# Blocks 1 to 7 of x: transposed by DMA as 16-bit halves and joined by GpSimd, in place of TensorE transposes

## The reference, cut to what matters

```python
x = x + L0(x)            # recurrent layer, below
x = x + L1(x)            # one linear layer, its weights chosen per batch row by an index
x = L2(x)                # adapter (512 -> 128 -> 512, relu) added to x, then a layer norm
x = x + L3(x)            # one linear layer, chosen per batch row
# L0:
ctx    = ema(x, tau)                              # over time, per channel
wg     = sigmoid([x, ctx] @ Wg.T + bg);  gated = x * wg
mod    = 0.5 + sigmoid(gelu(x @ Wn1.T) @ Wn2.T)   # two rows per token
trace_d = ema(gated * mod_d, tau_d)               # d = 0, 1
temporal = blend of the two traces
out    = (gelu(x @ Wsoma.T) * sigmoid(temporal @ Wtemp.T)) @ Wout.T
L0     = layernorm(out)
```

## Time and profile before

| what | value |
|---|---|
| median of 3 runs | 788.96 us (787.5 to 789.58) |
| the profiled execution | 787.42 us |
| its span, first to last instruction | 785.6 us |
| PE, DVE, ACT, POOL busy | 98%, 68%, 41%, 13% of the span |

### The profile page before, as it was taken

One profiled execution on the slowest core, in us unless ns is written; L12 is line 12 of the kernel. 1 busy time (PEld: TensorE's weight loads), 2 busy tenths in 40 slices (PEclk: granted clock), 3 DMA queues, 4 the chain that ended last, 5 costly groups with the idle time before them and its releaser, 6 DMA issues. The chain is left out here.

```text
span 785.6 us, 10804 instructions
## 1 busy us (share of the span) xinstructions
PE 767.6 (98%) x3628; PEld 628.3 (80%) x3628; DVE 533.8 (68%) x782; ACT 323.8 (41%) x525; POOL 101.4 (13%) x227
## 2 busy tenths in 40 slices
PE   5999999999999999999999999998999999999997
PEld 4888888888888888888888888776888888888885
DVE  3598894694695595595596587746775776657645
ACT  4444426226225315315325424656453544535332
POOL 2000020021012003003003004324001020110110
PEclk9999999999999999999999999999999999999999
DMA  7413004004004004102102514443142241313102
GB/s 222 167 55 108 27 1 161 28 0 161 27 0 160 27 0 146 41 0 111 76 0 81 136 53 157 146 146 141 41 148 70 105 147 41 121 63 111 40 28 82
DMA packets 32480, 66.29 MB, mean 84 GB/s; under 512 B 10800, under 2 KB 11824, under 8 KB 30400
## 3 DMA queue, kind: packets, MB, share of 16 engines
q1 hardware_dynamic: 32224, 65.87, 24.2%
q0 software_dynamic: 224, 0.00, 0.0%
HBM read 40.67 MB, written 25.20 MB: 84 GB/s over the span
## 5 line engine op out<-in xcount | busy, mean ns | idle before, releaser
L557 PE MATMUL pc<-x_h,wg_h 128*128 128x512 f32 x224 | 89.2, 398 | 0.0
L559 PE MATMUL pc<-x_h,wg_l 128*128 128x512 f32 x224 | 88.0, 393 | 0.0
L558 PE MATMUL pc<-x_l,wg_h 128*128 128x512 f32 x224 | 87.2, 389 | 0.0
L1292 DVE TENSOR_TENSOR_SCAN stage_b<-alpha,carry,stage_b 128x512 f32<-128x512 f32 x64 | 78.4, 1267 | 0.0
L999 ACT ACTIVATE ctx_t<-ctx_t,col_bg 128x512 f32<-128x512 f32 x32 | 23.2, 724 | 97.4 <-DVE ctx_t L1272 97.4
L1227 DVE TENSOR_TENSOR x_l<-x_t,x_h 128x512 fp32r<-128x512 f32 x32 | 22.2, 692 | 47.5 <-ACT x_t L949 47.5
L653 PE MATMUL pm<-t_h,wt_h 128*128 128x512 f32 x128 | 51.4, 402 | 0.0
L557 PE MATMUL pm<-wo_h,s_h 128*128 128x512 f32 x128 | 50.6, 395 | 0.7 <-DVE s_l L1251 0.7
L559 PE MATMUL pm<-wo_h,s_l 128*128 128x512 f32 x128 | 50.5, 394 | 0.0
L558 PE MATMUL pm<-wo_l,s_h 128*128 128x512 f32 x128 | 50.4, 394 | 0.0
L655 PE MATMUL pm<-t_h,wt_l 128*128 128x512 f32 x128 | 50.3, 393 | 0.0
(11 more groups left out here) (226 smaller groups left out, 1881.1 us busy)
## 6 DMA issues: line engine op xcount, KB each, us to landing
xt_scratch<-x_t SPq DMA_DIRECT2D x8, 1024.0 KB, 4.0
n_scratch<-stage_a SPq DMA_DIRECT2D x8, 1024.0 KB, 4.7
ctx_t<-xt_scratch SPq DMA_DIRECT2D x16, 512.0 KB, 6.4
x_tok<-in_x_dram SPq DMA_DIRECT2D x30, 256.0 KB, 2.8
out_dram<-x_tok SPq DMA_DIRECT2D x28, 256.0 KB, 2.0
s_h<-n_scratch SPq DMA_DIRECT2D x12, 512.0 KB, 4.9
mod<-mod_scratch SPq DMA_DIRECT2D x8, 512.0 KB, 3.5
stage_b<-in_L_cond_weight_dram SPq DMA_DIRECT2D x2, 1024.0 KB, 5.5
```

Source lines behind the costliest of these rows:

```text
L557: nc.tensor.matmul(acc, ah, bh, start=start and q == 0, stop=False)
L558: nc.tensor.matmul(acc, ah, bl, start=False, stop=False)
L559: last = nc.tensor.matmul(acc, al, bh, start=False, stop=stop and q == n - 1)
L1292: nc.vector.tensor_tensor_scan(tr[:, m % 2, :], alpha[:, 1 + d:2 + d].to_broadcast([P, BLK]), tr[:, m % 2, :], carry[:, D - d, m:m + 1], A ...
```

## The change

Only block 0 is still transposed by TensorE. For block i+1, SP issues one DMA transpose of its 512 by 1024 halves (16 bits each) from DRAM into `x_pairs`, in which even partitions hold the low halves and odd partitions the high halves of a channel (`turn_x` of SP). Four DMAs within SBUF sort them into `x_planes` (`spread_x`). GpSimd then reads a chunk's two planes and writes them as whole words into `x_t`, with one 1024-element copy of 16-bit elements (`weave_x`), behind a small instruction that writes `gone`. ScalarE makes `x_h` from `x_t` in four instructions a block in place of eight, and VectorE makes `x_l` chunk by chunk. The copy of chunk c may start when `gate_x(i, c)` has read the old chunk and the old block is stored. `c_h`, `c_l` of phase 2 are gone; x2's parts go to `t_h`, `t_l` for block 0 and to `s_h`, `s_l` for the others, and the normalised rows are read back into `x_pairs` and `x_planes`.

```diff
+    x_halves = t["x"].rearrange("b n e -> (b n) e").bitcast(U16)
-        c_h, c_l = sb("c_h", [P, NC, BLK], F32R), sb("c_l", [P, NC, BLK], F32R)
+        x_pairs, x_planes = sb("x_pairs", [P, NC, BLK]), sb("x_planes", [P, NC, BLK])
+        gone = sb("gone", [P, NC])
...
+        def x2_parts_of(i):
+            return (t_h, t_l) if isinstance(i, int) and i == 0 else (s_h, s_l)
...
+            def turn_x(i):
+                after(sp, x_spread, (i - 1) * 64)
+                sp.dma_start(pairs16, x_halves[bass.ds(i * BLK, BLK), :], transpose=True).then_inc(x_turned, 16)
+
+            def spread_x(i):
+                sp.wait_ge(x_turned, i * 16)
+                after(sp, x_woven, (i - 1) * NC)
+                for half in range(2):
+                    for s in range(2):
+                        sp.dma_start(planes16[64 * s:64 * s + 64, :, half, :],
+                                     pairs16[half::2, s::2, :]).then_inc(x_spread, 16)
...
             def step(i):
-                load_x(i + 1, 0)
-                load_x(i + 1, 1)
+                turn_x(i + 1)
                 store_xt(i)
+                spread_x(i + 1)
                 spread_mod(i)
-                load_x(i + 1, 2)
-                load_x(i + 1, 3)
                 store_n(i - 1)
...
+            def weave_x(i, c):
+                pool.wait_ge(x_spread, i * 64)
+                pool.wait_ge(xt_out, i * 16)
+                pool.wait_ge(gated, i * NC + (c + 1 - NC))
+                nc.gpsimd.tensor_tensor(gone[:, c:c + 1], keep[:, 0:1], keep[:, 1:2], ALU.mult)
+                nc.gpsimd.tensor_copy(words16[:, c, :, :], planes16[:, c, :, :].rearrange(
+                    "p w q -> p q w")).then_inc(x_woven, 1)
...
             def step(i):
-                temp_product(i - 1, (0, 1))
-                turn_x(i, 2)
-                turn_x(i, 3)
-                temp_product(i - 1, (2, 3))
+                temp_product(i - 1, range(NC))
                 h1_product(i)
...
+            def x_hi_part(i, c):
+                act.wait_ge(x_woven, i * NC + (c + 1 - NC))
+                if c == 0:
+                    act.wait_ge(soma_mm, i * NC)
+                nc.scalar.activation(x_h[:, c, :], x_t[:, c, :], ACT.Identity).then_inc(xcopy, 1)
...
                 norm_stats(i - 1, 1)
-                scan_traces(i, 2)
                 norm_stats(i - 1, 2)
                 norm_stats(i - 1, 3)
+                scan_traces(i, 2)
                 temporal_lo(i, 1)
```

More of the change, by code:

```diff
@@ L262, in store_xt @@
             def store_xt(i):
-                sp.wait_ge(xcopy, i * TILES + TILES)
+                if isinstance(i, int) and i == 0:
+                    sp.wait_ge(xcopy, TILES)
+                else:
+                    sp.wait_ge(x_woven, i * NC)
                 sp.dma_start(block_of(xt_scratch, i), x_t[:, :, :]).then_inc(xt_out, 16)
@@ L372, in _ @@
                         sp.dma_start(seq[n][:, b, :], cols_of(t[src], lang(b))).then_inc(lw_in, 16)
[L373 to L378, removed]
+            sp.wait_ge(x_spread, LAST * 64)
+            sp.wait_ge(n_out, 32)
+            for half in range(2):
+                load_n_half(0, x_pairs[:, 2 * half:2 * half + 2, :], half)
+            for half in range(2):
+                load_n_half(1, x_planes[:, 2 * half:2 * half + 2, :], half)
             spread_mod(LAST)
@@ L450, in _, with norm_scale @@
             pool.wait_ge(pool_step, 5)
-            def norm_scale(at, j, have_mv, done):
+            def norm_scale(at, j, have_mv, done, between=None):
                 v, y, q = newton[:, 0, :], newton[:, 1, :], newton[:, 2, :]
@@ L490, in carry_traces, with step @@
                                         ALU.mult).then_inc(tr_carry, 1)
-            def step(i, first=False, ends=False):
+            def weave_x(i, c):
[5 more added lines that the diff above has]
+                    "p w q -> p q w")).then_inc(x_woven, 1)
+            def step(i, first=False, ends=False, last=False):
                 k = 0 if ends else 1
                 carry_context(i, k)
[L496 to L500, removed]
+                carry_traces(i, 0, k)
+                if not last:
+                    weave_x(i + 1, 0)
+                    weave_x(i + 1, 1)
+                carry_traces(i, 1, k)
+                if not last:
+                    weave_x(i + 1, 2)
+                if first:
+                    weave_x(i + 1, 3)
+                    carry_traces(i, 2, k)
+                else:
+                    norm1_scale(i - 1, lambda: carry_traces(i, 2, k))
+                carry_traces(i, 3, k)
+                if not (first or last):
+                    weave_x(i + 1, 3)
             pool.wait_ge(setup_v, 4)
@@ L506, in _ @@
             step(PER_SEQ - 1, ends=True)
-            with pool.Fori(PER_SEQ, NBLK) as i:
+            with pool.Fori(PER_SEQ, LAST) as i:
                 step(i)
+            step(LAST, last=True)
             def add_eye(chunks, first, eye):
@@ L589, in ready, with turn_x @@
                 pe.wait_ge(w_lo, W_BEFORE[n] + W_COUNT[n])
[L591 to L599, removed]
+            def turn_x(k):
+                pe.wait_ge(x_in[k] if k < 2 else first_in[k - 2], 16)
                 if k >= 2:
-                    pe.wait_ge(xcopy, i * TILES + (k - 1))
-                src = x_first(k) if isinstance(i, int) and i == 0 else x_tok[:, k % 2, :]
-                turn(pt[k % 2], [src[:, out_cols(c)] for c in range(NC)]).then_inc(tx_done, 1)
+                    pe.wait_ge(xcopy, k - 1)
+                turn(pt[k % 2], [x_first(k)[:, out_cols(c)] for c in range(NC)]).then_inc(tx_done, 1)
             def of_x(wh, wl, at, o):
@@ L617, in u_chunk @@
             def u_chunk(i, m):
+                if m == 0:
+                    after(pe, soma_g, i * NC - 2)
                 if m == 1:
@@ L733, in _ @@
             step_end(1, first=True)
-            next_x(1)
-            with pe.Fori(2, LAST) as i:
+            with pe.Fori(2, NBLK) as i:
                 step(i)
-                next_x(i)
-            step(LAST)
             def turn_l3(b, k, bank):
@@ L779, in w1_product @@
                 wh, wl = w1_w(b)
+                c_h, c_l = x2_parts_of(i)
                 pairs = [(wh[:, c, :], wl[:, c, :], c_h[:, c, :], c_l[:, c, :]) for c in range(NC)]
@@ L1029, in traces_part @@
                 soma_gelu(i, 3)
-                if not last:
-                    copy_x(i + 1, 0)
                 temporal_hi(i, 3)
                 if not last:
-                    copy_x(i + 1, 1)
+                    for c in range(NC):
+                        x_hi_part(i + 1, c)
             def step(i, last=False):
-                copy_x(i, 2)
-                copy_x(i, 3)
                 gates(i - 1, lambda: hidden(i))
@@ L1342, in traces_part @@
                 blend_traces(i, 3)
-                if not last:
-                    x_lo_part(i + 1, 0)
                 temporal_lo(i, 3)
                 if not last:
-                    x_lo_part(i + 1, 1)
+                    for c in range(NC):
+                        x_lo_chunk(i + 1, c)
             def step(i, last=False):
-                x_lo_part(i, 2)
-                x_lo_part(i, 3)
                 gates(i - 1, lambda: hidden_lo(i))
```

108 lines of the change are left out of this document (48 added, 60 removed).

## The result

The changed kernel takes 798.37 us in the median (4 runs, 797.18 to 798.74), the kernel before 788.23 (4 runs, 785.42 to 789.58): a ratio of 1.0124, with a 95% interval of 1.0106 to 1.0143. It is 1.2% slower: the direction was forecast, but it is 10 us and not 50. The profiled execution took 798.66 us, its span 796.9.

The account below looks back on a forecast made before the run. PE, busy 98%, was taken as the bound, beside a second chain as long as the step (slack 1.0 us). 787.4 + 37.5 + 8.1 − 0.9 = 832.1 us, with the clock 839; range 775 to 866.

Parts of the forecast that it names:

- The price of the copy, w: Time of one 1024-element GpSimd copy, taken as 2.9 us, with bounds of 1.3 and 4.8.
- The sum's form: Whole kernel time as 768.3 + 22w, without the clock loss; 832.1 us at the forecast w.
- The turns: TensorE transposes of x: 0.88 us a group, 14 groups removed, 12.3 us saved if nothing else moves; PE step 58.8.
- Mutual exclusion: A VectorE instruction with two SBUF inputs and a GpSimd one reading SBUF block each other for a whole instruction.
- The first rival: GpSimd's copies share freely with VectorE; 9.9 us saved, 777.5 us; chance 0.14.
- The chain: Work freeing PE's banks each step: copies +3w − 0.5, scans −2.46, norm_scale +2.3 to 2.4; together 3w − 0.6 longer.
- The wait forecast on the banks: PE waits 3w − 0.7 = 8.0 us each step on banks normalise1 empties; step 66.8 us, +37.5 over steps 1 to 6.
- Block 0: Block 1's first h1_product waits for x_l through four copies, starting at 73.8 instead of 65.7: +8.1 us.
- The clock: PE's clock drops after waits: 1 us for each of seven, +7 us; bounds nothing to 17 us.
- DMAs at nothing: The transpose and four sorting DMAs are covered by about 21 us before spread_mod and cost nothing.
- The sign: Whole kernel: slower 0.82, same 0.03, faster 0.15; under exclusion, faster needs w < 0.87.
- a short copy: GpSimd's copy takes w = 1.3 with exclusion and no clock term: 797 us; chance 0.12.

Follow-up runs that it names:

- kernel before without turns: The kernel before with only the TensorE transposes of blocks 1 to 7 of x left out, ScalarE's copies kept: 778.78 us, ratio 0.988.
- the fill: The changed kernel with each GpSimd copy replaced by a memset of the same 1024 elements, which reads nothing: 779.71 us, ratio 0.9888.
- set back: The changed kernel with chunk 2's scans again ahead of the last two statistics and the third carry ahead of norm_scale's chain: 800.62 us, ratio 1.017.
- the half copy: The changed kernel with each GpSimd copy cut to 512 of its 1024 elements: 785.76 us, ratio 0.9966.
- the contiguous one: The changed kernel with each copy taking 1024 contiguous halves of a weight buffer in place of pairs from two planes: 793.26 us.
- the late copies: The changed kernel with all four copies behind norm_scale's chain and the last carry from step 1 on, block 0 unchanged: 782.01 us, ratio 0.9928.
- the words: The changed kernel with each copy taking 512 words of 32 bits from a weight buffer in place of 1024 halves: 783.6 us.

## Why the prediction was wrong, step by step

- **The price of the copy, w**, is the step that failed. "By elements the copy takes 1.30 + 512 × 0.00219 = 2.42 us" took its slope from two-input subtractions; the copy, with one input and no arithmetic, takes 0.96 ns an element in place of 2.19, and w is 1.15 in place of 2.9. The lower bound, 1.3, lay above the truth. On top I put 0.5 us for the alternating pairs, measured 0.12. The error is 1.75 us a copy, 22 × 1.75 = 38 us of the forecast.
- **The sum's form** held. With w = 1.15 it gives 768.3 + 25.3 = 793.6; with three dips of 1.6 it gives 798.4, and the profiled execution took 798.7. That the agreement is this close is luck: each step came out at 61.1 and not at 58.1 + 3w = 61.55, and behind the last step 1.2 us came on top of the dip.
- **The turns**: 1.65 us a step for two groups (kernel before without turns), forecast 1.76 (with 0.09 us for a gap that is 0.31 − 0.23 = 0.08); the PE step without them was forecast at 58.8 and is 58.9. Right.
- **Mutual exclusion**: right, and for a one-input copy too (0.77 to 0.97 us lost for each copy of 1.15). The first rival, a copy that shares freely at 777.5, is out. It was the right thing to ask: the fill, which doesn't hold VectorE up, gives 779.7.
- **The chain**: forecast "+3w − 0.5" for the copies, measured 2.7 of 3.45, so −0.75; forecast 2.3 to 2.4 for `norm_scale` beside the scans, measured 1.95. The scans' −2.46 and that nearly cancel, as forecast (set back, the step is 0.45 longer). The wait forecast on the banks, 3w − 0.7, would be 2.75 at w = 1.15; the step's 61.14 − 58.85 = 2.3.
- **Block 0**: the forecast had h1_product wait for `x_l` until 62.2 + 4w, 66.8 at w = 1.15. The last `x_l` is done at 67.22, close to that, but PE doesn't wait for it. PE waits for `t_l` of chunk 1, which the same copies delay, and with the dip behind that wait it comes to h1_product at 68.42. The size of this term is nearly right, the wait is another one.
- **The clock**: 7 us in seven waits forecast. In the profile it was 1.6 in each of three, two of them behind the longest waits of phase 1 and one in phase 2, where I had put nothing. The waits of 1.5 us lose none.
- **DMAs at nothing**: right in phase 1. The changed kernel without copies is 1.0 us from the kernel before without turns, and that is what phase 2 lost, where the forecast said that the renamed buffers cost nothing; what in phase 2 costs it was not tested. The transpose took 7.8 us from the start of its issue to the end of SP's wait for it, 5.8 of them the issue. The estimate of 4 us for 1 MB from the 261 GB/s of the Trainium skill, "DMA: Bandwidth & Descriptors", section on latency and measured facts, is for the transfer alone, which the trace doesn't show apart.
- The Trainium skill, "GPSIMD Engine Reference", section on performance pitfalls, would have put 50% on each element read at a step over 8 bytes. The innermost pair here is 1 KB apart, and the runs show 12%.
- **The sign** needed w > 0.87. Between the half copy (0.66 us: 785.8, faster) and the contiguous one (1.03: 793.3, slower) the kernel crosses 788 at w of about 0.77. The rival "a short copy", 797 at w = 1.3, was the case that came. That it is only 1.4 us off in time is luck: the dips, which it excluded for short waits, made up for its long w. Its chance of 0.12 was too small: of the two bounds of w, I had leaned on the one scaled up from a dearer kind of instruction.

## What to carry to other kernels

Price an instruction by a row of the same operation with the same number of inputs, not only of the same engine and size: on GpSimd a subtraction of two inputs took more than twice the time of a copy of as many elements. Work moved to a nearly idle engine isn't free if it reads SBUF beside VectorE's two-input instructions; its length then lies on VectorE's chain. Look at which chain that is: the 28 copies cost 18.6 us in front of the statistics, and with 24 of them moved behind about 2 us were left, so the place decides more than the count. And look at the mean granted clock of each execution before reading a difference of a few us: one profile without a dip isn't a kernel without dips.

## What the hardware showed that was not expected

- A GpSimd fill of 1024 halves (0.95 us) beside VectorE's two-input instructions delays nothing, while a copy of 1.03 us costs them 0.65 to 0.84 and one of 1.15 us 0.77 to 0.97.
- A GpSimd copy goes by elements more than by bytes: 0.60 us for 512 words, 0.66 for 512 halves, 1.03 for 1024 halves. So joining halves (1.15) costs nearly twice what copying the same bytes as words would.
- PE's clock dips last 3.4 us, 1.6 us lost each, or 6.8 (for instance in phase 2 of the half copies, the late copies and the words). They don't follow the length of the wait alone. A wait of 2.46 us on `t_l` has one behind it in the changed kernel, and the same 2.5 us with the late copies has none. With each copy made twice, five step boundaries in one execution have waits of 2.95 to 3.02 us, and the second and fourth have a dip, the others none. What decides it was not found.
